# Two of every eight C products on VectorE, out of PSUM, and layer norm statistics on ScalarE, in a decoder layer with a Mamba scan

## The chip, the cores and the metric

The kernel runs on one core of one Trainium2 chip. The metric is the device time of one execution in microseconds (us). A core has a matrix engine (TensorE, PE in the profile, its weight loads PEld), VectorE (DVE), ScalarE (ACT), GpSimd (POOL) and SyncE (SP), which here only issues DMAs. Each engine works through its own queue in order; they meet through semaphores. SBUF and PSUM are the on-chip memories; PSUM has 8 banks of 512 f32 in each of 128 partitions.

## What is computed

A layer on x (64 sequences x 128 positions x 512): a Mamba mixer, banded attention gated by a context, and eight small experts of which two are chosen, each behind a layer norm and added to x.

```python
x = x + mamba(layernorm(x))
x = x + attention(layernorm(x), ctx)
x = x + experts(layernorm(x))

def layernorm(x): return (x - mean(x)) / sqrt(var(x) + 1e-5)

def mamba(x):                      # I = 1024 channels, N = 16 states
    h_in, gate = split(x @ in_proj_w.T)
    u  = silu(causal_conv4(h_in) + conv_b)
    ts, Bm, Cm = split(u @ x_proj_w.T)
    dt = softplus(ts @ dt_proj_w.T + dt_proj_b)
    # for each channel and state, over the 128 positions t:
    # h[t] = exp(dt[t] * A) * h[t-1] + dt[t] * u[t] * Bm[t]
    y  = sum_over_states(h * Cm) + D * u
    return (y * silu(gate)) @ out_proj_w.T
```

## The kernel before

Sequences go in pairs (a group g of GB = 2), 32 groups; a tile is 128 x 512 f32. The work is a software pipeline: one pass, `iteration(g, cur, nxt, p1, p2)`, carries four groups at once: the scans of group g (`cur`), norm, projections and convolution of group g+1 (`nxt`), output projection and attention of group g-1 (`p1`) and the experts of group g-2 (`p2`). Each engine has its own `iteration`, a list of calls written out by hand whose order is the order of the engine's queue; passes 2 to 29 run in a loop of two passes.

The scan is the core of it. A pass has 64 steps s, each for 128 channels (chunk `s // 8`) and two of the 16 states, over two sequences:

- ScalarE, `decays` (L462): two exponentials write exp(dt A) into PSUM bank `s % 2` (DAR = 2), all but column 0 of each sequence, which stays zero so that the scan restarts there. It waits for `h_done` of step s-2, whose decays had the bank.
- GpSimd, `times_b` (L300), the B product: writes dt u B into the ring slot `s % 8` of SBUF, once TensorE has used the slot (`hc_used`).
- VectorE, `scan` (L1454): reads the decays (PSUM) and the ring slot, and leaves the states in the ring slot.
- the C product, states times C, in place in the ring slot, `times_c`: on VectorE (L1439) for the steps in `DVE_C`, those with s % 8 in (1, 4, 7), 24 of 64; on GpSimd (L309) for the other 40.
- TensorE, `y_sum` (L1066): adds the ring slots, transposed, two steps at a time, into PSUM bank 2; `y_turn`, `y_back` and `out_proj` (L1087, L526, L1096) turn the gated result and project it.

Around that, VectorE has the four steps of the softplus and du (`soft_step`, L1423 to L1434), the convolution's taps (`conv`, L1582), the row maxima and products of attention (L1489, L1496, L1503, L1507, L1513), the router, and the statistics of the three layer norms a, t and e (`norm_stats`: bn_stats over 512, bn_aggr, add of eps; L1403 to L1408) for two tiles each. `hold` is a tiny copy that stands between a wait and an instruction that takes none. After the statistics GpSimd raises to the power -1/2 (`rstd`, L288), VectorE makes the shift (`shift`, L1413) and ScalarE normalises (L469).

ScalarE has besides the decays the copies out of PSUM, the softplus's exponential and logarithm, the attention's exponentials and the silus. Exponential, logarithm and silu lie in different function tables; a change of table is an ACT_TABLE_LOAD. PSUM bank 3 (PS_B) serves projections, gates and transposes in turn; banks 4 to 7 (PS_ATT) serve attention, output projection and experts. SyncE's queue loads x, the context (`context`), the weight pieces and the rows of B and C (`spread`).

Of the kernel before, what the change touches and what calls it, by code (L numbers as in the profile page):

```python
# [5 lines left out]
def decoder_layer(nc, x_d, ctx_d, w_in_d, conv_w_d, conv_b_d, w_xt_d, w_xbc_d, w_dt_d, dt_b_d, a_log_d,  # L6
# [9 lines left out]
    P = 128  # L16
# [22 lines left out]
    DVE_C = [s for s in range(64) if s % 8 in (1, 4, 7)]  # L39
# [7 lines left out]
    with stack:  # L47
# [33 lines left out]
        held = sb("held", [P, 1])  # L81
# [29 lines left out]
        ln_st = {k: sb("ln_st_" + k, [P, GB, 6]) for k in "ate"}  # L111
        ln_mv = {k: sb("ln_mv_" + k, [P, GB, 2]) for k in "ate"}
# [31 lines left out]
        st_open, bo_ps, bo_done, att_zero = sem("st_open"), sem("bo_ps"), sem("bo_done"), sem("att_zero")  # L144
# [54 lines left out]
        def _(sp):  # L199
# [78 lines left out]
        def _(pool):  # L278
            nc.gpsimd.memset(neg_half[:], -0.5).then_inc(const_done, 1)
            nc.gpsimd.memset(v_aug[:, :, :, DH + 1:32], 0.0).then_inc(att_zero, 1)  # L280
            nc.gpsimd.memset(v_aug[:, :, :, DH:DH + 1], 1.0).then_inc(att_zero, 1)
            nc.gpsimd.memset(nmax[:], 0.0).then_inc(att_zero, 1)
            pool.wait_ge(const_done, 1)
# [29 lines left out]
            def iteration(g, cur, nxt, p1, p2):  # L313
                if cur:
                    times_b(g, 0)
                    times_b(g, 1)
# [4 lines left out]
                if p1:  # L321
                    times_c(g - 1, 62)
                if cur:
                    times_b(g, 3)
                    times_c(g, 0)
                    times_b(g, 4)
                    times_b(g, 5)
                    times_c(g, 2)
                    times_b(g, 6)
                    times_c(g, 3)  # L330
                    times_b(g, 7)
                if nxt:
                    rstd("a", g + 1, 0, 2)
                if p1:
                    rstd("t", g - 1, 0)
                if cur:
                    times_b(g, 8)
                    times_c(g, 5)
                    times_b(g, 9)
                    times_c(g, 6)  # L340
                    times_b(g, 10)
                    times_c(g, 8)
                    times_b(g, 11)
                    times_c(g, 10)
                    times_b(g, 12)
                    times_c(g, 11)
                if p1:
                    rstd("t", g - 1, 1)
                if cur:
                    times_b(g, 13)  # L350
                    times_b(g, 14)
                    times_b(g, 15)
                    times_c(g, 13)
                    times_b(g, 16)
                    times_b(g, 17)
                    times_b(g, 18)
                    times_c(g, 14)
                    times_b(g, 19)
                    times_c(g, 16)
                    times_b(g, 20)  # L360
                    times_c(g, 18)
# [3 lines left out]
                    times_c(g, 19)  # L365
                    times_c(g, 21)
                    times_b(g, 24)
                    times_b(g, 25)
                    times_b(g, 26)
                    times_b(g, 27)  # L370
                    times_c(g, 22)
                    times_b(g, 28)
                    times_b(g, 29)
                    times_c(g, 24)
                    times_c(g, 26)
                    times_b(g, 30)
                    times_c(g, 27)
                    times_b(g, 31)
                    times_c(g, 29)
                    times_c(g, 30)  # L380
                    times_b(g, 32)
                    times_b(g, 33)
                    times_b(g, 34)
                    times_b(g, 35)
                    times_b(g, 36)
                    times_b(g, 37)
                    times_b(g, 38)
                    times_c(g, 32)
                    times_c(g, 34)
                    times_c(g, 35)  # L390
                    times_b(g, 39)
# [4 lines left out]
                    times_b(g, 43)  # L396
                    times_b(g, 44)
                    times_c(g, 38)
                    times_b(g, 45)
                    times_c(g, 40)  # L400
                    times_b(g, 46)
                    times_b(g, 47)
                    times_c(g, 42)
                    times_c(g, 43)
                    times_c(g, 45)
                    times_b(g, 48)
                    times_c(g, 46)
                    times_b(g, 49)
                    times_b(g, 50)
                    times_b(g, 51)  # L410
                    times_c(g, 48)
                    times_b(g, 52)
                    times_c(g, 50)
                    times_b(g, 53)
                    times_c(g, 51)
                    times_b(g, 54)
                    times_b(g, 55)
                    times_c(g, 53)
                    times_b(g, 56)
# [6 lines left out]
                    times_b(g, 61)  # L426
                    times_c(g, 58)
                    times_c(g, 59)
# [16 lines left out]
        def _(act):  # L445
# [7 lines left out]
            act.wait_ge(da_zeroed, 1)  # L453

            def decays(g, s):

                ic, r = s // RS, s % RS
                if s % (2 * RS) == 0:
                    act.wait_ge(dt_done, g * NQ + ic // 2 + 1)
                act.wait_ge(h_done, g * SG + s + 1)  # L460
                for n in (2 * r, 2 * r + 1):
# [3 lines left out]
                        scale=a_neg[:, ic, n:n + 1]).then_inc(da_done, 1)  # L465

# [16 lines left out]
            def step_size(j, q):  # L483

                reached(act, du_done, (j - 1) * NQ + q + 1)
                act.wait_ge(dt_ps, j * NQ + q + 1)
# [124 lines left out]
            def iteration(g, cur, nxt, p1, p2):  # L611
                j = g + 1
                if cur:
                    decays(g, 0)
                    decays(g, 1)
                    step_size(g, 3)
                if p2:
                    experts_norm(g - 2, 0)
                if cur:
                    decays(g, 2)  # L620
                if p2:
                    experts_norm(g - 2, 1)
                if cur:
                    decays(g, 3)
# [1285 lines left out]
```

## Time and profile before

| | us |
|---|---|
| median of 3 runs | 5537.23 |
| lowest, highest | 5533.24, 5540.6 |
| the profiled execution | 5533.42 |
| its span in the trace | 5531.6 |
| busy in the span: TensorE / VectorE / GpSimd / ScalarE | 4796.2 / 4955.4 / 4541.5 / 4058.8 |
| TensorE weight loads | 3435.7 |
| mean granted TensorE clock | 0.964 |

The profile is of one execution. Busy times of an engine can be set against the length of a stretch; an idle time is put down to the instruction whose semaphore came last. In names of groups the arrow points from the inputs to the output, and "x" gives the number of instructions. Consecutive instructions of an engine overlap a little, so the steps between starts are shorter than the durations.

### The profile page before, as it was taken

What the parts mean: (1) busy time and instruction counts of PE and PEld (TensorE: products, weight loads), DVE (VectorE), ACT (ScalarE), POOL (GpSimd) and SP (SyncE); (2) the same over time, 40 slices, a digit from 0 to 9 for tenths busy, and PEclk for the clock granted to TensorE, in tenths of its full rate; (3) what the DMA queues carried; (4) which work ended last, traced back from release to release, by engine and by line L of the source; (5) the groups of instructions that cost most, each with busy time, mean ns of one, the idle gap of its engine ahead of it and who ended that gap; (6) DMA issues with size and microseconds to landing.
All of it is one profiled execution on the core that took longest, in us unless ns stands there. A gap on an engine that the chain in (4) does not pass through costs nothing.

```text
span 5531.6 us, 139169 instructions
## 1 busy us (share of the span) xinstructions
PE 4796.2 (87%) x51012; PEld 3435.7 (62%) x51012; DVE 4955.4 (90%) x7075; ACT 4058.8 (73%) x7812; POOL 4541.5 (82%) x3464
## 2 busy tenths in 40 slices
PE   5788888988888988888989888989888988898876
PEld 3566666666666666666666666666666666666653
DVE  3999999999999999999999999999999999999972
ACT  3677777877777777777877777777777777777752
POOL 2988888888888888888888888888888888888870
PEclk8899999999999999999999999999999999999986
DMA  3211222221212221212221222221212221221100
GB/s 112 71 63 42 70 68 74 70 66 42 74 64 74 70 67 41 74 64 74 71 67 40 74 64 74 74 70 34 77 64 70 74 74 38 70 69 66 62 9 11
DMA packets 114693, 350.19 MB, mean 63 GB/s; under 512 B 13057, under 2 KB 14849, under 8 KB 113921
## 3 DMA queue, kind: packets, MB, share of 16 engines
q1 hardware_dynamic: 114048, 341.51, 19.0%
q8 instruction: 416, 6.82, 0.5%
q14 instruction: 229, 1.87, 0.1%
HBM read 323.64 MB, written 17.83 MB: 62 GB/s over the span
## 4 chain that ended last, share of the span: by engine, by line
PE 46%; DVE 18%; issue 15%; POOL 11%; ACT 7%; DVEq 1%; POOLq 0%; ACTq 0%
POOL ring L300 7%; PE ps L1066 7%; PE ps L1114 6%; DVE ring L1454 5%; PE ps L1096 5%; PE ps L982 4%; PE ps L957 4%; POOL ring L309 4%; PE ps L1134 3%; PE ps L1010 3%; DVE nmax L1489 3%; ACT ps L462 3%; DVE ring L1439 2%; DVE tmp L1423 2%; PE ps L1021 1%
## 5 line engine op out<-in xcount | busy, mean ns | idle before, releaser
L300 POOL TENSOR_TENSOR ring<-du,bc 128x512 f32<-128x512 f32 x2048 | 2741.9, 1356 | 577.7 <-PE ps L1066 352.3
L1454 DVE TENSOR_TENSOR_SCAN ring<-ps,ring 128x512 f32<-128x512 f32 x2048 | 2456.7, 1211 | 201.2 <-POOL ring L300 103.1
L462 ACT ACTIVATE ps<-delta,a_neg 128x254 f32<-128x254 f32 x4096 | 1761.5, 468 | 326.9 <-DVE ring L1454 320.9
L309 POOL TENSOR_TENSOR ring<-ring,bc 128x512 f32<-128x512 f32 x1280 | 1776.5, 1394 | 232.5 <-DVE ring L1454 230.6
L1066 PE MATMUL ps<-ident,ring 128*128 128x128 f32 x8192 | 1103.7, 282 | 73.7 <-DVE ring L1439 43.1
L1066 PEld LDWEIGHTS ps<-ident,ring 128*128 128x128 f32 x8192 | 962.9, 145 | 193.5 <-issue 119.1
L1439 DVE TENSOR_TENSOR ring<-ring,bc 128x512 f32<-128x512 f32 x768 | 755.4, 987 | 3.4
L592 ACT ACTIVATE probs_mem<-ps 128x768 f32<-128x768 f32 (+1 forms) x512 | 455.9, 911 | 176.0 <-PE ps L1010 174.4
L1134 PE MATMUL ps<-w_in,xt_a 128*128 128x256 f32 x2048 | 488.8, 394 | 12.8 <-DVE hc L1582 8.1
L1114 PE MATMUL ps<-xt_a,w_in 128*128 128x256 f32 x2048 | 476.6, 386 | 7.1 <-DVE hc L1582 4.1
L1096 PE MATMUL ps<-w_outp,yz 128*128 128x512 f32 x1024 | 462.5, 599 | 18.7 <-ACT yz L526 18.7
L1489 DVE TENSOR_REDUCE nmax<-ps 128x8 f32<-128x1280 f32 x256 | 380.7, 1487 | 78.4 <-PE ps L982 73.8
L1134 PEld LDWEIGHTS ps<-w_in,xt_a 128*128 128x128 f32 x2048 | 398.1, 200 | 68.4 <-DVE hc L1582 8.9
L1114 PEld LDWEIGHTS ps<-xt_a,w_in 128*128 128x128 f32 x2048 | 381.6, 191 | 76.7 <-issue 17.7
L1582 DVE SCALAR_TENSOR_TENSOR hc<-ps,conv_w,hc 128x254 f32<-128x254 f32 (+2 forms) x768 | 363.1, 473 | 62.2 <-ACT hc L537 42.7
L1096 PEld LDWEIGHTS ps<-w_outp,yz 128*128 128x128 f32 x1024 | 190.1, 191 | 227.9 <-issue 199.8
L982 PE MATMUL ps<-qk 32*32 32x160 f32 (+2 forms) x16384 | 296.2, 297 | 0.0
L1010 PE MATMUL ps<-qk 32*128 32x192 f32 (+1 forms) x4096 | 286.8, 397 | 0.0
L1021 PE MATMUL ps<-probs_mem,v_aug 128*32 128x192 f32 (+1 forms) x4096 | 229.8, 367 | 44.0 <-ACT probs_mem L592 43.9
L579 ACT ACTIVATE qk<-ps,b_qk 128x512 f32<-128x512 f32 x256 | 170.6, 678 | 125.6 <-PE ps L957 125.6
L957 PE MATMUL ps<-xb,w_qk 128*128 128x512 f32 x512 | 241.1, 593 | 2.8 <-ACT qk L579 1.3
L1010 PEld LDWEIGHTS ps<-qk 32*128 32x128 f32 x4096 | 186.3, 197 | 68.4 <-issue 63.1
(136 smaller groups left out, 6362.2 us busy)
## 6 DMA issues: line engine op xcount, KB each, us to landing
w_in<-in_w_in SPq DMA_DIRECT2D x256, 512.0 KB, 3.7
bc<-bc_rows SPq DMA_DIRECT2D x256, 512.0 KB, 4.1
x_new<-in_x SPq DMA_DIRECT2D x32, 512.0 KB, 6.2
x_res<-in_x SPq DMA_DIRECT2D x32, 512.0 KB, 5.5
enc<-in_ctx SPq DMA_DIRECT2D x64, 256.0 KB, 5.3
out<-x_att SPq DMA_DIRECT2D x32, 512.0 KB, 2.8
w_outp<-in_w_outp SPq DMA_DIRECT2D x1, 2048.0 KB, 8.0
bc_rows<-bc_sb SPq DMA_DIRECT2D x32, 32.0 KB, 1.5
```

Source lines behind the costliest of these rows:

```text
L300: nc.gpsimd.tensor_tensor(ring[:, s % RING, :].rearrange("p (n t) -> p n t", n=2), du[:, q % 2, (ic % 2) * NT:(ic % 2 + 1) * NT].rearrange ...
L309: nc.gpsimd.tensor_tensor(ring[:, s % RING, :], ring[:, s % RING, :], bc[:, s % RS, 2:4, :].rearrange("p a t -> p (a t)"), ALU.mult).then_ ...
L462: nc.scalar.activation(ps[:, s % DAR, (n % 2) * NT:(n % 2 + 1) * NT].rearrange("p (b t) -> p b t", b=GB)[:, :, 1:T], delta[:, ic, :].rearr ...
L982: last = nc.tensor.matmul(ps[32 * a:32 * a + 32, PS_ATT + hp, j * NEAR + lo:j * NEAR + hi], qk[r:r + 32, j, n * P + 32 * a:n * P + 32 * a ...
L1010: last = nc.tensor.matmul(ps[:, PS_ATT + hp, a * WIN + lo:a * WIN + hi], qk[r:r + 32, 2 + j, blk * P:(blk + 1) * P], qk[r:r + 32, j, at:at ...
L1066: last = nc.tensor.matmul(ps[:, PS_Y, b * T:(b + 1) * T], ring[:, t % RING, n * NT + b * T:n * NT + (b + 1) * T], ident[:], start=False, s ...
L1096: last = nc.tensor.matmul(ps[:, PS_ATT + b, :], yz[:, ic, b * T:(b + 1) * T], w_outp[:, ic, :], start=(ic == 0), stop=(ic == NI - 1))
L1114: last = nc.tensor.matmul(ps[:, PS_B, a * NT:(a + 1) * NT], w_in[:, slot, k, a * P:(a + 1) * P], xt_a[:, k, :], start=(k == 0), stop=(k == ...
L1134: last = nc.tensor.matmul(ps[:, PS_B, b * NT:(b + 1) * NT], xt_a[:, k, b * T:(b + 1) * T], w_in[:, slot, k, :], start=(k == 0), stop=(k == ...
L1439: nc.vector.tensor_tensor(ring[:, s % RING, :], ring[:, s % RING, :], bc[:, s % RS, 2:4, :].rearrange("p a t -> p (a t)"), ALU.mult).then_ ...
L1454: nc.vector.tensor_tensor_scan(ring[:, s % RING, :], ps[:, s % DAR, :], ring[:, s % RING, :], 0.0, ALU.mult, ALU.add).then_inc(h_done, 1)
L1489: nc.vector.tensor_reduce(nmax[:, n].rearrange("p j (a r) -> p a j r", r=32)[:, :, :, DH], ps[:, PS_ATT:PS_ATT + 4, 0:NJ * NEAR].rearrange ...
```

## The change

`DVE_C` becomes the steps with s % 8 in (3, 7), 16 of 64; GpSimd makes the other 48. For these 16 steps the scan leaves its states in the PSUM bank of the decays, over the decays, and VectorE's C product reads them there and writes the ring slot. Two steps later the bank takes decays again: ScalarE now waits for the C product (`hcd_done`) and first writes zeros back into the four first columns (`nc.scalar.copy`).

The statistics of the layer norms leave VectorE. The sum over a row comes as a second output (`accum_out`) of the additions that VectorE makes anyway (t and e), and for a from a pass of ScalarE over the tile (`total`). ScalarE squares the tile against its sum (`squares`; it writes into PS_B for a, into PS_ATT + b for t, into the context's buffer for e) and makes variance plus eps (`variance`). TensorE's first projection of attention waits for the squares of t, the load of the next context for those of e. The two copies in the router that only signal are made smaller. All `iteration` lists are written anew.

```diff
-    DVE_C = [s for s in range(64) if s % 8 in (1, 4, 7)]
+    DVE_C = [s for s in range(64) if s % 8 in (3, 7)]
...
             def context(i):
-                reached(sp, enc_used, i)
+                reached(sp, ln_aggr["e"], i)
...
             def decays(g, s):
...
+                if (s - DAR) % SG in DVE_C:
+
+                    reached(act, hcd_done, g * NDC + dvc(s - DAR + 1) if s >= DAR else (g - 1) * NDC + dvc(s - DAR + SG + 1))
+                    nc.scalar.copy(ps[:, s % DAR, :].rearrange("p (k t) -> p k t", t=T)[:, :, 0:1],
+                                   zeros[:].rearrange("p (k o) -> p k o", o=1)).then_inc(da_reset, 1)
                 act.wait_ge(h_done, g * SG + s + 1)
...
+            def total(j, b):
+                act.wait_ge(x_in, (j + 1) * 16)
+                nc.scalar.activation(x_new[:, b, :], x_new[:, b, :], ACT.Identity,
+                                     accum_out=ln_sum["a"][:, b:b + 1]).then_inc(ln_stat["a"], 1)
+
+            def squares(use, g, b):
+
+                i = g * GB + b
+                if use == "a":
+                    reached(act, yz_done, (g - 1) * NI)
+                    reached(act, gate_done, g * NQ)
+                    if b:
+                        act.wait_ge(ln_aggr["a"], i)
+                src = {"a": x_new, "t": x_res, "e": x_att}[use]
+                act.wait_ge({"a": ln_stat["a"], "t": x1_done, "e": x2_done}[use], i + 1)
+                nc.scalar.activation({"a": ps[:, PS_B, :], "t": ps[:, PS_ATT + b, :], "e": enc[:]}[use], src[:, b, :], ACT.Square,
+                                     scale=-float(H), bias=ln_sum[use][:, b:b + 1],
+                                     accum_out=ln_var[use][:, b:b + 1]).then_inc(ln_aggr[use], 1)
+
+            def variance(use, g, b):
+                act.wait_ge(ln_aggr[use], g * GB + b + 1)
+                nc.scalar.activation(ln_rs[use][:, b:b + 1], ln_var[use][:, b:b + 1], ACT.Identity,
+                                     scale=1.0 / H ** 3, bias=eps[:]).then_inc(ln_eps[use], 1)
...
                     if n == 0:
                         pe.wait_ge(xb_done, i + 1)
-                        pe.wait_ge(x1_done, g * GB)
+                        pe.wait_ge(ln_aggr["t"], g * GB)
...
             def times_c(g, s):
                 dve.wait_ge(h_done, H0 + 1 + g * SG + s)
-                nc.vector.tensor_tensor(ring[:, s % RING, :], ring[:, s % RING, :],
+                nc.vector.tensor_tensor(ring[:, s % RING, :], ps[:, s % DAR, :],
...
-                nc.vector.tensor_tensor_scan(ring[:, s % RING, :], ps[:, s % DAR, :], ring[:, s % RING, :], 0.0,
+                state = ps[:, s % DAR, :] if s in DVE_C else ring[:, s % RING, :]
+                nc.vector.tensor_tensor_scan(state, ps[:, s % DAR, :], ring[:, s % RING, :], 0.0,
...
-                nc.vector.tensor_tensor(x_res[:, b, :], ps[:, PS_ATT + b, :], x_res[:, b, :], ALU.add).then_inc(x1_done, 1)
+                nc.vector.scalar_tensor_tensor(x_res[:, b, :], ps[:, PS_ATT + b, :], 1.0, x_res[:, b, :], ALU.mult, ALU.add,
+                                               accum_out=ln_sum["t"][:, b:b + 1]).then_inc(x1_done, 1)
```

In VectorE's list of scans 47 to 56, for instance, the C products stood as 47, 49 (after scan 53), 52 (after 54) and 55; now 47, 51 and 55 each stand right behind their own scan.

The order on VectorE in a pass of the loop, from scan 2 on. The scan reads as SCALAR_TENSOR_TENSOR here; ISA and REGISTER_ALU rows prepare or make a wait. Before:

```order
L1454 SCALAR_TENSOR_TENSOR ring<-ps,ring 128x512 [waits dbx_done,da_done]
L1452 REGISTER_ALU
L1454 SCALAR_TENSOR_TENSOR ring<-ps,ring 128x512 [waits dbx_done,da_done]
L1482 ISA
L1403 BN_STATS ln_st_a<-x_new 128x6 [waits x_in]
L1404 ISA
L1399 COPY held<-neg_half 128x1 [waits ln_stat_a]
L1406 BN_AGGR ln_mv_a<-ln_st_a 128x2
L1408 TENSOR_SCALAR ln_rs_a<-ln_mv_a 128x1 [waits ln_aggr_a]
L1452 ISA
L1454 SCALAR_TENSOR_TENSOR ring<-ps,ring 128x512 [waits dbx_done,da_done]
```

Now:

```order
L1532 SCALAR_TENSOR_TENSOR ring<-ps,ring 128x512 [waits dbx_done,da_done]
L1529 ISA
L1532 SCALAR_TENSOR_TENSOR ps<-ps,ring 128x512 [waits dbx_done,da_done]
L1515 REGISTER_ALU
L1516 TENSOR_TENSOR ring<-ps,bc 128x512 [waits h_done]
L1529 ISA
L1532 SCALAR_TENSOR_TENSOR ring<-ps,ring 128x512 [waits dbx_done,da_done]
L1529 REGISTER_ALU
L1532 SCALAR_TENSOR_TENSOR ring<-ps,ring 128x512 [waits dbx_done,da_done]
L1545 REGISTER_ALU
L1546 REGISTER_ALU [waits xres_in]
L1547 SCALAR_TENSOR_TENSOR x_res,ln_sum_t<-ps,x_res 128x512 [waits outp_ps]
```

Between scans 3 and 4 the statistics of x_new are gone and a C product out of PSUM stands there, right behind its scan, which writes ps.

The order on ScalarE at the softplus's logarithm and the experts' silu, between the decays of steps 8 and 9. Before:

```order
L512 ACT_TABLE_LOAD
L512 ACTIVATE lnv<-soft 128x512
L609 ACT_TABLE_LOAD
L609 ACTIVATE probs_mem<-ps 128x256
L460 REGISTER_ALU
L462 ACT_TABLE_LOAD
L462 ACTIVATE ps<-delta,a_neg 128x2x127 x2
```

Now, with the reset of the bank that step 7's states had:

```order
L556 ACT_TABLE_LOAD
L556 ACTIVATE lnv<-soft 128x512
L507 ACTIVATE ln_rs_a<-ln_var_a,eps 128x1
L198 REGISTER_ALU
L477 COPY ps<-zeros 128x4
L479 REGISTER_ALU
L481 ACT_TABLE_LOAD
L481 ACTIVATE ps<-delta,a_neg 128x2x127 x2
```

The logarithm's load is followed by the exponentials' own load at once; the silu's load, which shared its change of table with it, now stands some rows further on with another pair.

The order on GpSimd in the same stretch, B products (ring<-du,bc) and C products (ring<-ring,bc). Before, from the B product of step 4 on:

```order
L299 REGISTER_ALU
L300 TENSOR_TENSOR ring<-du,bc 128x512
L299 REGISTER_ALU
L300 TENSOR_TENSOR ring<-du,bc 128x512
L309 TENSOR_TENSOR ring<-ring,bc 128x512
L299 REGISTER_ALU
L300 TENSOR_TENSOR ring<-du,bc 128x512
L309 TENSOR_TENSOR ring<-ring,bc 128x512
L299 REGISTER_ALU
L300 TENSOR_TENSOR ring<-du,bc 128x512
```

Now, from the B product of step 4 on too:

```order
L303 REGISTER_ALU
L304 TENSOR_TENSOR ring<-du,bc 128x512
L313 TENSOR_TENSOR ring<-ring,bc 128x512
L303 REGISTER_ALU
L304 TENSOR_TENSOR ring<-du,bc 128x512
L303 REGISTER_ALU
L304 TENSOR_TENSOR ring<-du,bc 128x512
L303 REGISTER_ALU
L304 TENSOR_TENSOR ring<-du,bc 128x512
L303 REGISTER_ALU
L304 TENSOR_TENSOR ring<-du,bc 128x512
L313 TENSOR_TENSOR ring<-ring,bc 128x512 x4
```

Before, B and C products alternate; now four B products stand ahead of four C products.

## Rows read from the trace of the kernel before

**Rows 1.** The page: busy time and share of the span, by engine.

```profile
PE 4796.2 (87%) x51012; PEld 3435.7 (62%) x51012; DVE 4955.4 (90%) x7075; ACT 4058.8 (73%) x7812; POOL 4541.5 (82%) x3464
```

**Rows 2.** Engines by stretch: start:end us, length, busy us (instructions), clock, DMA.

```profile
1009.80:1087.30 77.50, 66.64 (x569) 48.61 (x569) 72.47 (x92) 65.23 (x124) 65.10 (x49) 0.98 0.29 95
1087.30:1175.10 87.80, 80.67 (x1034) 57.44 (x1034) 82.61 (x131) 62.41 (x124) 77.68 (x62) 1.00 0.12 39
2000.00:3000.00 1000.00, 889.77 (x9716) 638.23 (x9716) 930.88 (x1334) 763.82 (x1470) 855.65 (x653) 0.98 0.20 65
```

**Rows 3.** The chain of waits, first and last of 25 pieces: start us, us.

```profile
927.63 6.97 PE ps L1096 x16
4897.35 6.97 PE ps L1096 x16
```

**Rows 4.** Waits between 1000 and 4968 us: us in total, times, longest us.

```profile
PE ps L928 <- DVE nmax L1489: 45.9, 72, 1.0
DVE ring L1454 <- POOL ring L300: 70.1, 93, 1.3
DVE ring L1454 <- ACT ps L462: 67.0, 69, 1.9
POOL ring L300 <- PE ps L1066: 278.2, 179, 4.4
POOL ring L309 <- DVE ring L1454: 174.7, 109, 2.6
ACT ps L462 <- DVE ring L1454: 212.0, 155, 2.0
```

**Rows 5.** Groups by line; behind the bar busy us, mean ns of one, then idle.

```profile
L300 POOL TENSOR_TENSOR ring<-du,bc 128x512 f32<-128x512 f32 x2048 | 2741.9, 1356 | 577.7 <-PE ps L1066 352.3 <-DVE du L1434 225.4
L1454 DVE TENSOR_TENSOR_SCAN ring<-ps,ring 128x512 f32<-128x512 f32 x2048 | 2456.7, 1211 | 201.2 <-POOL ring L300 103.1 <-ACT ps L462 94.2 <-issue 0.3
L309 POOL TENSOR_TENSOR ring<-ring,bc 128x512 f32<-128x512 f32 x1280 | 1776.5, 1394 | 232.5 <-DVE ring L1454 230.6
L1439 DVE TENSOR_TENSOR ring<-ring,bc 128x512 f32<-128x512 f32 x768 | 755.4, 987 | 3.4
L1423 DVE SCALAR_TENSOR_TENSOR tmp<-tmp,soft 128x512 f32<-128x512 f32 x128 | 174.6, 1364 | 19.6 <-ACT tmp L506 19.6
L1503 DVE TENSOR_TENSOR o_sb<-ps,o_sb 128x512 f32<-128x512 f32 x128 | 81.3, 675 | 3.7 <-PE ps L1040 3.7
L1513 DVE SCALAR_TENSOR_TENSOR x_att<-ps,b_ct,x_res 128x512 f32<-128x512 f32 x64 | 46.9, 733 | 4.1 <-PE ps L1050 4.1
```

**Rows 6.** Single lines of VectorE and GpSimd: duration ns min/median/max.

```profile
L1439 DVE TENSOR_TENSOR ring<-ring,bc x768: 657/693/1791, 106.5 to 5374.2; 128x512 f32<-128x512 f32 x192
L1503 DVE TENSOR_TENSOR o_sb<-ps,o_sb x128: 664/677/692, 320.2 to 5499.6; 128x512 f32<-128x512 f32 x128
L300 POOL TENSOR_TENSOR ring<-du,bc x2048: 1253/1275/1831, 99.5 to 5371.5; 128x512 f32<-128x512 f32 x187
L309 POOL TENSOR_TENSOR ring<-ring,bc x1280: 1253/1277/1772, 105.5 to 5373.9; 128x512 f32<-128x512 f32 x183
```

**Rows 7.** VectorE in order of time, statistics of one tile: start us, us.

```profile
1090.20 0.14 DVE L1399 COPY held<-neg_half 128x1 f32<-128x1 f32 x1
...
1091.36 0.69 DVE L1423 SCALAR_TENSOR_TENSOR tmp<-tmp,soft 128x512 f32<-128x512 f32 x1
```

**Rows 8.** ScalarE in order of time: start us, us.

```profile
1093.83 0.21 ACT L605 ACTIVATE small<-small 128x16 f32<-128x16 f32 x1 [4.07 <-DVE small L1538]
1093.95 0.85 ACT L462 ACTIVATE ps<-delta,a_neg 128x254 f32<-128x254 f32 x2
1094.82 1.28 ACT L512 ACT_TABLE_LOAD   x1
1096.11 0.63 ACT L512 ACTIVATE lnv<-soft 128x512 f32<-128x512 f32 x1
...
1100.56 0.80 ACT L469 ACTIVATE xb<-x_res,ln_nm_t,ln_rs_t 128x512 f32<-128x512 f32 x1
```

More of the change, by code:

```diff
@@ L614, in iteration @@
                     decays(g, 0)
+                    step_size(g, 3)
+                if nxt:
+                    total(j, 0)
+                if cur:
                     decays(g, 1)
-                    step_size(g, 3)
+                if nxt:
+                    total(j, 1)
+                if cur:
+                    decays(g, 2)
                 if p2:
@@ L619, in iteration @@
                 if cur:
-                    decays(g, 2)
+                    decays(g, 3)
                 if p2:
@@ L635, in iteration @@
                     decays(g, 6)
+                if nxt:
+                    squares("a", g + 1, 0)
                 if p2:
                     experts_x(g - 2, 1)
+                if nxt:
+                    squares("a", g + 1, 1)
                 if cur:
                     decays(g, 7)
+                if p1:
+                    squares("t", g - 1, 0)
+                if cur:
+                    soft_one(g, 2)
+                if nxt:
+                    variance("a", g + 1, 0)
+                if p1:
+                    variance("t", g - 1, 0)
+                if cur:
+                    decays(g, 8)
+                    soft_ln(g, 2)
+                if nxt:
+                    variance("a", g + 1, 1)
+                if cur:
+                    decays(g, 9)
                 if p2:
@@ L666, in iteration @@
                     attention(g, p2, 0, "v")
+                if cur:
+                    decays(g, 13)
                 if nxt:
@@ L730, in iteration @@
                     decays(g, 29)
+                    skip_term(g, 5)
+                    decays(g, 30)
+                    soft_one(g, 3)
+                    decays(g, 31)
                 if p1:
@@ L755, in iteration @@
                 if cur:
-                    skip_term(g, 5)
                     decays(g, 36)
+                if p1:
+                    attention(g, p2, 1, "v")
+                if cur:
                     decays(g, 37)
+                    decays(g, 38)
+                    decays(g, 39)
                 if nxt:
@@ L778, in iteration @@
                     attention(g, p2, 1, "exp", 0)
+                    squares("e", g - 1, 0)
                 if cur:
-                    decays(g, 44)
                     decays(g, 45)
-                    skip_term(g, 6)
                 if p1:
@@ L808, in iteration @@
                 if cur:
-                    decays(g, 51)
+                    decays(g, 48)
+                if p1:
+                    attention(g, p2, 1, "exp", 4)
+                if cur:
+                    decays(g, 49)
+                if p1:
+                    attention(g, p2, 1, "exp", 5)
+                if cur:
+                    decays(g, 50)
                 if nxt:
@@ L839, in iteration @@
                     decays(g, 57)
+                if p1:
+                    attention(g, p2, 1, "wide")
+                if nxt:
+                    step_size(j, 0)
+                if cur:
+                    decays(g, 58)
+                if nxt:
+                    soft_exp(j, 0)
+                if cur:
+                    decays(g, 59)
                 if nxt:
@@ L1684, in iteration @@
                     scan(g, 19)
+                    times_c(g, 19)
+                    y_step(g, 1)
+                    scan(g, 20)
                 if nxt:
```

583 lines of the change are left out of this document (271 added, 312 removed).

## The prediction

> **What bounds the kernel now.** I read the busy shares first: VectorE 4955 us of 5532, GpSimd 4542, ScalarE 4059, TensorE 4796 [rows 1]. Then the period: the long output projection comes once a pass, 24 passes lie between 927.63 and 4897.35, so one pass takes 165.4 us [rows 3]. The steady stretch from 2000 to 3000 us gives the load of a pass (times 0.1654): VectorE 154.0, TensorE 147.2, GpSimd 141.5, ScalarE 126.3 [rows 2]. VectorE is busy 93.1% of a pass and is what bounds it, closely followed.
>
> A pass has two halves. In the first (77.5 us) VectorE has 72.5, TensorE 66.6, ScalarE 65.2, GpSimd 65.1; in the second (87.8 us) VectorE has 82.6 and TensorE 80.7 [rows 2]. VectorE's own idle time before scans is 2.9 us a pass for GpSimd's B product and 2.8 for ScalarE's decays (70.1 and 67.0 over 24); GpSimd waits 11.6 for ring slots and 7.3 for scans, ScalarE 8.8 for scans, TensorE 1.9 for the row maxima [rows 4]. So the others mostly wait at VectorE's pace.
>
> **VectorE.** Today 24 C products of 987 ns; a product with one operand in PSUM takes 675 [rows 5]. The shortest C product takes 657 and the longest 1791, the PSUM one 664 to 692, and GpSimd's products stretch in the same way, from 1253 to 1831 [rows 6]: two engines hold each other up when VectorE reads two operands from SBUF. The change leaves 16 products, all with the state in PSUM: 24 x 0.987 - 16 x 0.675 = 12.9 us less. The statistics of a tile take 1.16 us (1090.20 to 1091.36) [rows 7], six a pass: 7.0 less. Added: sums written out by four additions; the nearest prices are 0.06 (733 against 675 [rows 5]) and a small instruction's 0.14 [rows 7], at least nothing: 0 to 0.6, I take 0.4. The scan's output moves to PSUM in 16 of 64 scans. No row shows VectorE writing 512 elements there; reading there costs 677 against 693 in the medians [rows 6], and the small gap 733 - 675 bounds it above: -0.3 to +1.0, taken as 0, since a scan is paced by its recurrence at 1211 [rows 5]. VectorE: 154.0 - 12.9 - 7.0 + 0.4 = 134.5. The router's two copies swapped for smaller ones are nothing.
>
> The Trainium skill speaks against the PSUM operand: "VectorE: DVE Perf Modes", section "The TRN2 errata", gives a VectorE read from PSUM 62 cycles more fixed cost than one from SBUF, by my estimate from its figures 1.0 us a pass. The medians 677 and 693 [rows 6] don't show it; by it the pass of VectorE would be 135.5 and still last.
>
> **GpSimd.** Eight more C products at the undisturbed 1.277 [rows 6]: +10.2. Its means exceed its medians by 64 x 0.081 + 40 x 0.117 = 9.9 a pass [rows 5, 6], time in which VectorE holds it up. VectorE's C products exceed 675 by 24 x 0.312 = 7.5, the first softplus step, which reads two SBUF operands too, by 4 x 0.689 = 2.8 [rows 5], the other steps by less; so I give two thirds of the 9.9, 6.6, to the C products, and it goes. GpSimd: 141.5 + 10.2 - 6.6 = 145.1, between 141.8 (all goes) and 151.7 (nothing goes).
>
> **ScalarE.** Added in a pass: 16 resets of the first decay column, 0.12 (start to start) to 0.21 each [rows 8], at 0.17: 2.7. Two sums at 0.63 and six squares at 0.80 like the passes over 512 elements [rows 8]: 6.1. Six variances at 0.21: 1.3. Table loads: the order in the loop has 24 for two passes before and 30 now, three more a pass at 1.29 (1094.82 to 1096.11) [rows 8]: 3.9. ScalarE: 126.3 + 14.0 = 140.3; reading the accumulators out is not in any row, nothing to 8 x 0.21 = 1.7 more.
>
> The Trainium skill, "ScalarE: Activation LUTs", section "What ACT_TABLE_LOAD costs", puts a drain of some 1.4 us behind each load; that would make it 8.0 for the three. The row has the next activation start 1.29 after the load began [rows 8], so I keep 3.9.
>
> **TensorE** keeps its work, 147.2. The added waits: the projection of the first batch waits for both squares of the mixer's sum, since they overwrite its two banks (before: for the additions only); behind it the rest of attention is queued. The prefetch of the context waits for the squares of the experts' input, with a weight piece and the spread rows behind it on SyncE's queue. Both are issued some ten or more scans ahead of their use and I price them at 0, at most 0.8 each, the length of a squares pass [rows 8], if the cover is gone.
>
> **The sum.** The order of load is now TensorE 147.2, GpSimd 145.1, ScalarE 140.3, VectorE 134.5. What comes last is no longer one engine. Two ways to a period: (a) TensorE as full as VectorE was, 147.2 / 0.931 = 158.1. (b) By halves with the old placing: first half ScalarE 65.2 + 7.0 = 72.2, at the old fullness 72.5 / 77.5 = 77.2 us; second half TensorE 80.7, at 82.6 / 87.8 = 85.8 us; together 163.0. The new order moves work between halves but four engines within 9% of each other leave less room to absorb waits. I take the middle, 160.5: 4.9 us a pass, 32 passes (2048 scans of 64) [rows 5], 157 us. Against the profiled execution of 5533.4 (span 5531.6): 5376; the median lies 3.8 above that, so **5380**.
>
> **Rivals.**
> (1) More: half of TensorE's idle 18.2 us goes too, since part of it is waits for VectorE (the row maxima [rows 4]). 147.2 + 9.1 = 156.3 a pass, 291 less: 5246. Against it: GpSimd would be 93% and ScalarE 90% full.
> (2) Less: the halves don't even out, 163.0 a pass, 77 less: 5460. For it: ScalarE gains most load and sits in the half where it becomes last.
> (3) The change doesn't do what it says: a C product with bc in SBUF is still held up. Then GpSimd has 151.7, and 151.7 / 0.931 = 162.9: 5457. The row of 664 to 692 [rows 6] speaks against it.
> (4) Slower: the two decay banks. A scan in PSUM keeps its bank until the C product has read it, and only then come the reset and both exponentials for the scan two ahead. The chain scan, decays, scan gets 0.68 + 0.17 = 0.85 longer in 16 places, and where ScalarE stands at a reset, everything behind it on its queue stands too: copies for TensorE, the exponentials of attention. Before, two exponentials (0.85 [rows 8]) hid behind the scan in between (1.21 [rows 5]); now 0.17 + 0.85 leaves about 0.2 for two hand-overs. What is uncovered adds to 160.5; from 4.9 / 16 = 0.31 us a product the kernel is slower. At 0.55 it is 8.8 a pass, 169.3: 5662. For it: at scans 47 to 55 of the new order nothing else lies between. Against it: VectorE has 26 us of room in 160.5.
>
> **Chances.** Forecast 0.48; (1) 0.14; (2) 0.17; (3) 0.03; a tie between (2) and (4), within 0.2% (about what a measurement of this kernel can tell from no change), 0.06; (4) 0.12. Faster 0.82, same 0.06, slower 0.12. The range reaches from just beyond (1) to the edge of no change, 5235 to 5525; it leaves out (4) and a tail of (1). The unknown costs lie inside: GpSimd's ends 141.8 to 151.7, at 93.1%, give 152 to 163 a pass.
>
> **What would show it.** C products at 0.67 to 0.70 with a short maximum; GpSimd's two means near 1.30; fifteen table loads a pass; VectorE's share near 84%, TensorE's 92%; the long projections 160.5 apart. (4) shows as ScalarE's wait before the reset and VectorE's before scans <- ScalarE well over 2.8 us a pass. The forecast is wrong if the PSUM scan costs over 1.3, or if ScalarE waits more than before at decays and reset together.

## The result, and the profile after

The changed kernel takes 5381.8 us (5376.4 to 5387.6, four runs), before 5535.2 (5531.2 to 5540.6): ratio 0.9722, 95% interval 0.9706 to 0.9739. It is faster by 2.8%, and within 2 us of the forecast. Several of the forecast's steps were wrong all the same, and the runs below show which.

The page of the changed kernel, span and busy time by engine, against [rows 1]:

```profile
span 5385.8 us, 140112 instructions
PE 4741.3 (88%) x51012; PEld 3415.9 (63%) x51012; DVE 4558.6 (85%) x6051; ACT 4440.9 (82%) x9121; POOL 4640.2 (86%) x3722
```

VectorE has lost 397 us, ScalarE has gained 382, GpSimd only 99 although it makes eight more C products a pass. The length of a pass is again the distance between two long projections in the chain of waits of the changed kernel (start us, us), four passes apart:

```profile
4207.13 3.65 PE ps L1219 x16
...
4847.82 3.65 PE ps L1219 x16
```

640.69 / 4 = 160.2 us, where [rows 3] gave 165.4. The loads per thousand microseconds between 1000 and 4000 us, the view of [rows 2]:

```profile
sum 3000.00, PE 2733.41 PEld 1975.59 DVE 2647.92 ACT 2598.14 POOL 2716.39; mean PE 911.14 PEld 658.53 DVE 882.64 ACT 866.05 POOL 905.46
```

Times 0.1602, a pass holds TensorE 146.0, GpSimd 145.1, VectorE 141.4, ScalarE 138.7 us. The four lie within some 5%. TensorE's busy time has fallen too, from 4796.2 to 4741.3 us for the same 51012 matmuls; nothing in the change takes work off it.

The groups of the changed kernel that answer to [rows 5] (busy us, mean ns of one, then idle before and its releasers):

```profile
L304 POOL TENSOR_TENSOR ring<-du,bc 128x512 f32<-128x512 f32 x2048 | 2630.2, 1299 | 369.3 <-PE ps L1151 262.8
L1532 DVE TENSOR_TENSOR_SCAN ring<-ps,ring 128x512 f32<-128x512 f32 x1536 | 1851.4, 1212 | 285.3 <-ACT ps L481 251.3
L313 POOL TENSOR_TENSOR ring<-ring,bc 128x512 f32<-128x512 f32 x1536 | 2012.0, 1320 | 90.7 <-DVE ring L1532 87.8
L1532 DVE TENSOR_TENSOR_SCAN ps<-ps,ring 128x512 f32<-128x512 f32 x512 | 623.2, 1217 | 49.4 <-ACT ps L481 43.6
L1516 DVE TENSOR_TENSOR ring<-ps,bc 128x512 f32<-128x512 f32 x512 | 350.2, 684 | 9.9
L1500 DVE SCALAR_TENSOR_TENSOR tmp<-tmp,soft 128x512 f32<-128x512 f32 x128 | 236.1, 1845 | 26.7 <-ACT tmp L550 25.7
```

VectorE's C product fell from 987 to 684 ns, GpSimd's B product from 1356 to 1299 and its C product from 1394 to 1320. A scan that writes PSUM takes 1217, one that writes SBUF 1212. The first softplus step (now L1500) got longer, 1845 against 1364. The same lines one by one (ns min/median/max), as in [rows 6]:

```profile
L1516 DVE TENSOR_TENSOR ring<-ps,bc x512: 665/691/693, 111.0 to 5223.7; 128x512 f32<-128x512 f32 x171
L304 POOL TENSOR_TENSOR ring<-du,bc x2048: 1252/1272/1807, 101.7 to 5221.0; 128x512 f32<-128x512 f32 x187
```

The longest C product is 693 ns, before 1791: no GpSimd product holds one up any more.

The waits of the changed kernel between 1000 and 4841 us, 24 passes (us in total, times, longest us):

```profile
PE ps L1013 <- DVE nmax L1554: 110.2, 98, 3.0
DVE ring L1532 <- ACT ps L481: 184.4, 239, 3.3
DVE ps L1532 <- ACT ps L481: 28.2, 43, 1.5
ACT ps L477 <- DVE ring L1516: 86.5, 120, 2.3
ACT ps L481 <- DVE ring L1532: 127.2, 120, 3.0
```

VectorE now waits 8.9 us a pass for decays ((184.4 + 28.2) / 24) where it waited 2.8 [rows 4], and ScalarE stands 3.6 at the new reset. TensorE's wait for the row maxima has risen from 1.9 to 4.6. ScalarE's waits at decays and reset together are 213.7 us, before 212.0 at the decays alone.

**Where the time went.** From the first scan to the last, 164.65 us a pass became 159.9, 151.5 us in 32 passes; what follows the last scan became 4.8 us longer (158.6 to 163.4). Seen from TensorE, the span is 145.8 us shorter, 90.9 of them idle time and 54.9 busy time.

### The profile page after: what moved, and what is told of

Same layout as the page of the kernel before. It is cut to its first block and busy times, and to the rows that moved or that the text cites. A ratio compares the mean times of both kernels' runs of the same rounds, so it can differ in the third digit from the quotient of the medians.

```text
span 5385.8 us, 140112 instructions
## 1 busy us (share of the span) xinstructions
PE 4741.3 (88%) x51012; PEld 3415.9 (63%) x51012; DVE 4558.6 (85%) x6051; ACT 4440.9 (82%) x9121; POOL 4640.2 (86%) x3722
## 5 line engine op out<-in xcount | busy, mean ns | idle before, releaser
L304 POOL TENSOR_TENSOR ring<-du,bc 128x512 f32<-128x512 f32 x2048 | 2630.2, 1299 | 369.3 <-PE ps L1151 262.8
L1532 DVE TENSOR_TENSOR_SCAN ring<-ps,ring 128x512 f32<-128x512 f32 x1536 | 1851.4, 1212 | 285.3 <-ACT ps L481 251.3
L313 POOL TENSOR_TENSOR ring<-ring,bc 128x512 f32<-128x512 f32 x1536 | 2012.0, 1320 | 90.7 <-DVE ring L1532 87.8
L1151 PEld LDWEIGHTS ps<-ident,ring 128*128 128x128 f32 x8192 | 950.5, 144 | 225.4 <-issue 117.7
L1532 DVE TENSOR_TENSOR_SCAN ps<-ps,ring 128x512 f32<-128x512 f32 x512 | 623.2, 1217 | 49.4 <-ACT ps L481 43.6
L1199 PE MATMUL ps<-xt_a,w_in 128*128 128x256 f32 x2048 | 478.1, 387 | 9.4 <-DVE hc L1647 4.1
L1181 PE MATMUL ps<-w_outp,yz 128*128 128x512 f32 x1024 | 480.3, 607 | 3.6 <-issue 2.2
L1516 DVE TENSOR_TENSOR ring<-ps,bc 128x512 f32<-128x512 f32 x512 | 350.2, 684 | 9.9
L1067 PE MATMUL ps<-qk 32*32 32x160 f32 (+2 forms) x16384 | 314.2, 316 | 1.7 <-issue 1.7
L1095 PE MATMUL ps<-qk 32*128 32x192 f32 (+1 forms) x4096 | 273.6, 382 | 0.0
L1500 DVE SCALAR_TENSOR_TENSOR tmp<-tmp,soft 128x512 f32<-128x512 f32 x128 | 236.1, 1845 | 26.7 <-ACT tmp L550 25.7
```

Source lines behind the costliest of these rows:

```text
L304: nc.gpsimd.tensor_tensor(ring[:, s % RING, :].rearrange("p (n t) -> p n t", n=2), du[:, q % 2, (ic % 2) * NT:(ic % 2 + 1) * NT].rearrange ...
L313: nc.gpsimd.tensor_tensor(ring[:, s % RING, :], ring[:, s % RING, :], bc[:, s % RS, 2:4, :].rearrange("p a t -> p (a t)"), ALU.mult).then_ ...
L1067: last = nc.tensor.matmul(ps[32 * a:32 * a + 32, PS_ATT + hp, j * NEAR + lo:j * NEAR + hi], qk[r:r + 32, j, n * P + 32 * a:n * P + 32 * a ...
L1151: last = nc.tensor.matmul(ps[:, PS_Y, b * T:(b + 1) * T], ring[:, t % RING, n * NT + b * T:n * NT + (b + 1) * T], ident[:], start=False, s ...
L1181: last = nc.tensor.matmul(ps[:, PS_ATT + b, :], yz[:, ic, b * T:(b + 1) * T], w_outp[:, ic, :], start=(ic == 0), stop=(ic == NI - 1))
L1199: last = nc.tensor.matmul(ps[:, PS_B, a * NT:(a + 1) * NT], w_in[:, slot, k, a * P:(a + 1) * P], xt_a[:, k, :], start=(k == 0), stop=(k == ...
```

## The experiments

My theory was the forecast's: the C product out of PSUM ends the mutual hold-up of VectorE and GpSimd, the statistics give the rest, and VectorE was what bound the kernel before. The rival: another engine set the pace, and the loads of VectorE and GpSimd count only through what waits for them. The first four kernels take the change apart, the next six load one engine at a time, and the last two move the hand-over of the bank and the split of the products. All kernels compute the same outputs; those named "more" do extra work whose result nobody reads.

**The states back in SBUF**, without and with the reset and its wait. Two lines of the changed kernel; in the first kernel, `states_sbuf`, the five lines of the reset in `decays` go too:

```diff
-                nc.vector.tensor_tensor(ring[:, s % RING, :], ps[:, s % DAR, :],
+                nc.vector.tensor_tensor(ring[:, s % RING, :], ring[:, s % RING, :],
-                state = ps[:, s % DAR, :] if s in DVE_C else ring[:, s % RING, :]
+                state = ring[:, s % RING, :]
```

> The changed kernel with the 16 states back in SBUF: the scan writes the ring slot, VectorE's C product reads it there, and the reset and ScalarE's wait for the C product are gone. Theory (contention): VectorE's C product rises from 0.684 to about 0.99 us (some 5 us a pass), GpSimd's two means from 1.30 to about 1.35 (some 5 us a pass); the period grows by 2 to 4 us from 160.2, time 5450 to 5510. Rival (the bank chain costs what the PSUM operand saves): the chain reset, decays, scan is 0.85 shorter in 16 places, the two cancel, time within 15 us of 5382.

> As the one before, states in SBUF, but the reset and ScalarE's wait for the C product kept. Theory (the bank chain is covered, as VectorE has room): within 10 us of the one without them. Rival (the chain costs up to 0.85 us in 16 places): 50 to 300 us slower than the one without them.

Measured: `states_sbuf` 5520.1 us, ratio 0.9979 (0.9969 to 0.9988); `states_sbuf_reset` 5545.0, ratio 1.0022 (1.0012 to 1.0032). The page and two groups of `states_sbuf`:

```profile
PE 4801.6 (87%) x51012; PEld 3443.4 (62%) x51012; DVE 4779.1 (87%) x6051; ACT 4396.1 (80%) x8609; POOL 4909.2 (89%) x3722
L304 POOL TENSOR_TENSOR ring<-du,bc 128x512 f32<-128x512 f32 x2048 | 2770.4, 1368 | 294.2 <-PE ps L1146 194.3 <-DVE du L1506 99.4
L1511 DVE TENSOR_TENSOR ring<-ring,bc 128x512 f32<-128x512 f32 x512 | 688.4, 1345 | 9.9
```

The same 16 products take 1345 ns instead of 684, and GpSimd is busy 269 us longer with the same instructions. Nearly the whole gain, 138 us between these two kernels, hangs on where one operand lies. The loss is larger than expected, 5520 against 5450 to 5510, and so is the hold-up: 1345 ns where the kernel before had 987, so that part of what the operand saves is a hold-up that only the new order and split have. The hand-over of the decay bank costs a further 25 us (5520 to 5545) when the states gain nothing by it, more than the 10 that the theory allowed and less than the rival's 50.

The 138 us are not all waits. Of the 131.4 us between the two spans, TensorE's idle time has 71.1 (715.6 against 644.5) and its busy time 60.3 (4801.6 against 4741.3), for the same matmuls. The granted clock of its rows was 0.955 in `states_sbuf` and 0.965 in the changed kernel. A lower clock beside a longer busy time fits, but no run separates what the clock does from the rest.

**The statistics back on VectorE** (`stats_back`), and with it also the states in SBUF and no reset (`only_split`, which leaves of the change its order and the two products of eight). The statistics stand behind the additions of their tile, which lose their second output; the three ScalarE functions return at once, and TensorE and the context's load wait as in the kernel before:

```diff
+                nc.vector.bn_stats(ln_st[use][:, b, :], src[:, b, :]).then_inc(ln_stat[use], 1)
...
+                nc.vector.bn_aggr(ln_mv[use][:, b, :], ln_st[use][:, b, :]).then_inc(ln_aggr[use], 1)
...
+                nc.vector.tensor_scalar(ln_rs[use][:, b:b + 1], ln_mv[use][:, b, 1:2], EPS, None, ALU.add).then_inc(ln_eps[use], 1)
```

> The changed kernel with the layer norm statistics back on VectorE (bn_stats, bn_aggr and add of eps as before, placed behind the additions), none on ScalarE. Theory (no engine alone sets the period; VectorE at 142 of 160 has room for 7 us): between 10 us faster and 40 us slower than 5382. Rival 1 (ScalarE's 9 us a pass are on the path): 100 us or more faster. Rival 2 (VectorE still bounds through its waits): 7 us a pass, 220 us slower.

> Both undone: states in SBUF without reset, statistics on VectorE. What is left of the change is two of eight C products and the new order. Theory: VectorE near 154 again less 8 C products (147), GpSimd at 151 with the contention back: period 163 to 165, time 5470 to 5530. Rival (the gain is the order's): it stays within 30 us of 5382.

Measured: `stats_back` 5389.0, ratio 0.9738 (0.9722 to 0.9754); `only_split` 5514.3, ratio 0.9966 (0.9954 to 0.9977). So the change comes apart as: order and split 19 us, PSUM operand 125 (5514.3 to 5389.0), statistics 7, and these last can't be told from nothing, since the intervals overlap. With the states in SBUF, moving the statistics costs 6 instead (5514.3 to 5520.1). How the PSUM operand reaches the end of the program shows in TensorE's waits over the whole run, first of `only_split`, then of `stats_back`:

```profile
PE ps L1013 <- DVE nmax L1576: 211.1, 118, 4.4
PE ps L1151 <- DVE ring L1539: 73.5, 59, 1.7
```

```profile
PE ps L1018 <- DVE nmax L1581: 128.3, 126, 3.0
```

TensorE waits 83 us less for the row maxima of attention, which VectorE makes between its scans; all its waits together fall from 722 to 626. The other 30 us are again TensorE's busy time (4786.9 to 4757.2). A product held up makes VectorE late at the work that TensorE waits for. But GpSimd is relieved as well: the operand takes 214 us of busy time off VectorE (4893.4 to 4679.4) and 243 off GpSimd (4900.9 to 4657.6), and no run takes only one of the two.

**One engine loaded at a time, in the changed kernel.** VectorE gets six `bn_stats` a pass over a constant (`dve_more`), ScalarE 24 small activations (`act_more`), GpSimd six small products (`pool_more`), and TensorE the first of four matmuls of `h_in` twice (`pe_more`):

```diff
+                if s % 10 == 5:
+                    nc.vector.bn_stats(pad_st[:], w_outp[:, 0, :])
```

```diff
+                if s % 8 == 5:
+                    reached(act, pad_done, (g * 8 + s // 8) * 3)
+                    for i in range(3):
+                        nc.scalar.activation(pad[:, 16 * i:16 * i + 16], ident[:, 0:16], ACT.Identity).then_inc(pad_done, 1)
```

```diff
+                if s % 10 == 5:
+                    nc.gpsimd.tensor_tensor(pad[:], pad[:], pad[:], ALU.mult)
```

```diff
-                    for k in range(KH):
+                    for n in range(-1, KH):
+                        k = max(n, 0)
...
+                                                xt_a[:, k, :], start=(k == 0), stop=(n in (-1, KH - 1)))
```

> The changed kernel with six bn_stats over a constant weight tile added to a pass on VectorE (behind scans 5, 15, ... 55), 0.60 each from start to start: 3.6 us a pass, 116 us in all, whose result nobody reads. Theory (the next in load sets the pace, TensorE and GpSimd; VectorE has 20 us of room): a third of it or less, 0 to 40 us. Rival (VectorE still sets it through the chain scan, C product, reset): 80 us or more.

> The changed kernel with 24 tiny activations added to a pass on ScalarE (three behind the decays of steps 5, 13, ... 61), about 0.13 each: 3.1 us a pass, 100 us in all. Theory: ScalarE follows, 20 to 60 us. Rival (ScalarE sets the pace through the decays): 80 us or more.

> The changed kernel with six 64-wide products of a constant added to a pass on GpSimd (behind the B products of steps 5, 15, ... 55), 0.6 each: 3.6 us a pass, 115 us in all. Theory (GpSimd, 90% busy and first in the chain of waits, sets the pace with TensorE): 60 to 115 us. Rival (TensorE alone): under 30 us.

> The changed kernel with the first of the four weight rows multiplied twice in the convolution's projection (the first result is overwritten): eight 128x256 products of f32 a pass at 0.45, 3.6 us a pass, 115 us in all. Theory (TensorE, 91% busy, sets the pace with GpSimd): 60 to 115 us. Rival (GpSimd alone): under 30 us.

Measured, ratio to before: VectorE 0.9777 (0.9761 to 0.9794), ScalarE 0.9768 (0.9752 to 0.9784), GpSimd 0.9777 (0.9761 to 0.9794), TensorE 0.9918 (0.99 to 0.9935). The added groups, of `dve_more`, `act_more` and `pe_more` in turn (`pe_more` has 2560 of the last, the changed kernel 2048 and 478.1 us):

```profile
L1538 DVE BATCH_NORM_STATS2 pad_st<-w_outp 128x6 f32<-128x512 f32 x192 | 128.1, 667 | 0.0
```

```profile
L491 ACT ACTIVATE pad<-ident 128x16 f32<-128x16 f32 x768 | 106.2, 204 | 0.0
```

```profile
L1200 PE MATMUL ps<-xt_a,w_in 128*128 128x256 f32 x2560 | 587.8, 385 | 8.1 <-DVE hc L1648 4.1 <-ACT gate_t L595 2.6 <-ACT xt_a L574 0.8
```

Against the changed kernel's 0.9722, VectorE's 128 us cost 30, ScalarE's 106 cost 25, GpSimd's 58 cost 30 (each difference has some 13 us either way), and TensorE's 110 us cost 108. GpSimd's lands at its rival's bound (under 30, expected 60 to 115); the other three lie in the ranges of the theory. Only TensorE passes its work on whole, or nearly: its busy time rose by 124 us in all, VectorE's by 99, so that by these totals the shares are 0.9 and 0.3. TensorE's work was added in one place, ahead of a projection that others wait for, the work of the others was spread over the pass; a second place on TensorE was not tried.

**The same in the kernel before** (`before_dve_more`, `before_pe_more`; the edits are those above).

> The kernel before with the same six bn_stats a pass on VectorE (99 us of busy time in the changed kernel, where they cost 27). Theory (VectorE bounded the kernel before): 70 to 120 us slower than before, 5605 to 5655. Rival (TensorE bounded it already): under 40 us.

> The kernel before with the same doubled first products on TensorE (124 us of busy time in the changed kernel, where they cost 103). Theory (VectorE bounded it, TensorE had 18 us of room a pass): 20 to 70 us slower than before. Rival (TensorE bounded it already): 90 us or more.

Measured: 1.0088 (1.0072 to 1.0105) and 1.0205 (1.0188 to 1.0222): VectorE's 127.6 us of added work cost 49 us, TensorE's 110.5 cost 113. These are the runs that my theory fails on: I had expected 70 to 120 from VectorE and 20 to 70 from TensorE. The engine that was 93% busy passed 0.4 of its load on, the one that was 89% busy all of it. The page of the kernel before had a sign of it, the shares of the chain of work that ended last:

```profile
PE 46%; DVE 18%; issue 15%; POOL 11%; ACT 7%; DVEq 1%; POOLq 0%; ACTq 0%
```

**The decay bank uncovered** (`c_late`). Each of the 16 C products stands behind the scan that follows its own, so the bank is handed over one scan later; the other 15 calls go as the one shown, and no work is added. Only 12 of them move: those of steps 15, 27 and 31 stand there in the changed kernel too, and 63, the last of the pass, stays behind its own scan.

```diff
+                if s - 1 in DVE_C:
+                    times_c(g, s - 1)
+                if s == 63 and 1:
+                    times_c(g, 63)
...
-                    times_c(g, 3)
+                    pass
```

> The changed kernel with VectorE's 16 C products each behind the next scan instead of their own (63 at the pass's end). The bank's chain C product, reset, two exponentials then starts 1.2 us later and nothing covers it: VectorE waits about 1.1 us before 15 scans, 16 us a pass. Theory (the chain costs only what VectorE's room of 18 us and its slope of a quarter let through): 80 to 250 us slower than 5382. Rival (ScalarE stands at the reset and holds up TensorE's copies too): 300 us or more.

Measured: 5781.5, ratio 1.0452 (1.0435 to 1.047), 400 us over the changed kernel, more than the 80 to 250 expected, or 1.04 for each of the 12 products that moved. ScalarE's and VectorE's waits in it, over the whole run (in the changed kernel 134.5 us at the reset and 294.9 before scans):

```profile
ACT ps L477 <- DVE ring L1516: 565.1, 386, 6.0
```

```profile
L1532 DVE TENSOR_TENSOR_SCAN ring<-ps,ring 128x512 f32<-128x512 f32 x1536 | 1856.3, 1214 | 662.1 <-ACT ps L481 641.3 <-POOL ring L304 8.3 <-issue 3.7
```

With the scans into PSUM, VectorE's wait for decays is 734.9 us in `c_late`. The fourth rival's mechanism is real, and larger than the 0.85 that the forecast gave as its whole length. VectorE was busy 78% of the span, and its room did not help: the scans wait one after another, and room elsewhere does not shorten a chain.

**Five of sixteen C products on VectorE** (`dve_20`: 20 instead of 16 of 64), to see whether the fuller GpSimd holds the kernel.

```diff
-    DVE_C = [s for s in range(64) if s % 8 in (3, 7)]
+    DVE_C = [s for s in range(64) if s % 8 in (3, 7) or s % 16 == 5]
...
+                if s in DVE_C and s % 4 != 3:
+                    times_c(g, s)
```

> A version that may be better: VectorE makes 20 of 64 C products out of PSUM, those with s % 16 == 5 too, right behind their scans; GpSimd makes 44. By the slopes measured (VectorE 0.27, GpSimd 0.52, ScalarE 0.31 of what is added or taken): a pass +0.7 - 2.7 + 0.2 = -1.8 us, 56 us less, 5325. Rival (TensorE sets the pace and the places of the four are no good for the bank's chain): within 15 us of 5382 or slower.

Measured: 5401.7, ratio 0.976 (0.9744 to 0.9776), 20 us slower than the changed kernel where a gain of 56 was expected. The page and GpSimd's first group:

```profile
PE 4752.0 (88%) x51012; PEld 3418.7 (63%) x51012; DVE 4599.6 (85%) x6179; ACT 4453.8 (82%) x9249; POOL 4466.2 (82%) x3594
L304 POOL TENSOR_TENSOR ring<-du,bc 128x512 f32<-128x512 f32 x2048 | 2606.0, 1290 | 508.0 <-PE ps L1153 351.4 <-DVE du L1513 155.5
```

GpSimd is busy 174 us less and waits 139 us more (508.0 against 369.3): it used the room to wait, most of it for ring slots that TensorE empties. ScalarE's wait at the reset rose too, from 134.5 to 206.0 us (640 resets instead of 512), so the run does not say which of the two took the gain. (The trace is of the slowest of the four executions, 5424.6 us.) None of my kernels beats the changed one.

## Why the prediction was right, and where it was not

**The C product: right.** 684 ns against 675 forecast, and 693 at most. `states_sbuf` shows the other side, 1345. The row on which the step stood, a VectorE addition out of PSUM that was never longer than 692 [rows 6], carried over. The 62 cycles more of a PSUM read, in the Trainium skill's "VectorE: DVE Perf Modes", section "The TRN2 errata", don't show: the median is 691 here and was 693 from SBUF [rows 6].

**The scan into PSUM: right**, 5 ns more (1217 against 1212), 0.1 us a pass.

**GpSimd: right.** 145.1 forecast, 145.1 measured. The contention share too: 4909.2 - 4640.2 = 269 us between `states_sbuf` and the changed kernel is 8.4 a pass for 16 products of 1345 ns, against 6.6 forecast for 24 of 987.

**ScalarE: right**, 138.7 against 140.3. Its own rows, resets, table loads, sums with the new read-out of the accumulator, and variances, in the changed kernel:

```profile
L477 ACT COPY ps<-zeros 128x4 f32<-128x4 f32 x512 | 84.7, 165 | 134.9 <-DVE ring L1516 134.5
L481 ACT ACT_TABLE_LOAD x189 | 242.5, 1283 | 3.3
L488 ACT ACTIVATION_READ_ACCUMULATOR x_new<-x_new x64: 185/187/193, 19.6 to 4907.7; 128x1 f32 x64
L507 ACT ACTIVATE ln_rs_a<-ln_var_a,eps x64: 277/281/292, 21.9 to 4924.3; 128x1 f32<-128x1 f32 x64
```

The resets are 0.165 (0.17 forecast), the variances 0.28 (0.21), the read-out 0.19 for each of eight sums, 1.5 a pass, near the upper bound that was given; the squares took 0.69 instead of 0.80, which makes up for part of it. All table loads together are 479, fifteen a pass. Nothing stands behind a load: the logarithms, each of which follows one, sat idle 1.4 us before all 128 of them:

```profile
L556 ACT ACTIVATE lnv<-soft 128x512 f32<-128x512 f32 x128 | 80.7, 631 | 1.4
```

The drain of 1.4 us a load, in the Trainium skill's "ScalarE: Activation LUTs", section "What ACT_TABLE_LOAD costs", is not in this trace.

**VectorE: off by 6.9 us**, 141.4 instead of 134.5. The largest part, 4.4, is the softplus. Its later steps in the changed kernel (in the kernel before the four steps took 466.3 us together, now 236.1 for L1500 and these):

```profile
L1511 DVE TENSOR_TENSOR du<-delta,u 128x512 f32<-128x512 f32 x128 | 126.4, 988 | 0.0
L1503 DVE SCALAR_TENSOR_TENSOR delta<-delta,tmp 128x512 f32<-128x512 f32 x128 | 123.5, 965 | 0.0
L1507 DVE TENSOR_TENSOR delta<-delta,lnv 128x512 f32<-128x512 f32 x128 | 121.9, 952 | 2.7 <-ACT lnv L556 2.7
```

607.9 - 466.3 = 141.6 us, over 32 passes 4.4. They read two operands from SBUF, as the C product did; the forecast freed VectorE of the hold-up only where it removed it, and let it grow nowhere. It is not simply that GpSimd is fuller: the four steps took 473.2 us in `only_split`, where GpSimd is busy 4900.9, and 552.3 in `stats_back`, where it is busy 4657.6. What decides is not shown; which GpSimd products stand beside the steps changes with each kernel. A second part is the statistics. The 1.16 us of [rows 7] is start to start and holds gaps between small instructions, while a load is busy time: by `stats_back`, whose VectorE is busy 4679.4 us, they were worth about (120.8 + 55.6 for its shorter softplus + 10.5 for the accumulators) / 32 = 5.8 a pass, not 7.0. Of the last 1.3, the scans' busy time has 0.6 (2474.6 us against 2456.7); the rest I can't place.

**"VectorE bounds the kernel": wrong.** This is the step that failed. The forecast read it from the busy share and from the waits, and the added loads deny it (0.4 against 1.0, in the kernel before). The Trainium skill, "Perfetto Trace Analysis", section "Identifying the Most-Contended Engine", takes the engine of highest occupancy as the one to improve, which would have misled here as it misled me; of TensorE it says that its matmul busy share does not tell how close it is to its limit, and here the engine with the lower share was the one that passed its load on. So the 12.9 us a pass priced on VectorE's C products paid 19 and 125 us over 32 passes, 4.5 a pass (the 19 with the new order in them), in good part through the waits of TensorE, and the 5.8 of the statistics paid next to nothing: 7 us in all, by intervals that overlap.

**Why the sum came out.** Way (a) divided TensorE's 147.2 by a fullness, and TensorE is indeed what a pass is measured by; its fullness rose from 89% to 91%. Its load was kept at 147.2 without a second look and measured 146.0; over the run its busy time fell by 54.9 us, more than a third of the 145.8 that the span lost. At 91.1% the forecast's load would have given 161.6 a pass. That the fullness reached was between VectorE's old 93% and the halves' estimate was a middle taken between two ways, not a derivation. The ways lay 4.9 us a pass apart, 157 us in all, so that coming within 2 us of the total is partly luck, and VectorE's part in it had the wrong reason.

**Rivals.** (3) fell with the 693. (1) fell: TensorE's idle time is 14.2 us a pass and not 9.1. (2) was the nearer one, 163.0 against 160.2. (4), the decay bank, happened as described, but small: the hand-over cost 25 us in the form without its gain, 0.05 a product, where the forecast had the kernel slower from 0.31. Its signs were poor ones: VectorE's wait before scans rose from 2.8 to 8.9 a pass, and ScalarE's waits at decays and reset together are just over those of before (213.7 against 212.0 us), which the forecast named as proof that it was wrong; the time fell all the same. It stayed small where the C product stands ahead of the next scan, as 13 of the 16 do; `c_late` gives its price without that. The reason given against it, VectorE's room, was no reason.

**Not settled.** What of the 19 us of `only_split` is the new order and what the two products of eight was not run apart, nor was the lower fullness of TensorE divided between its many small waits. Open too are why TensorE is busy for less time with the same matmuls, and how much of the operand's gain comes by VectorE and how much by GpSimd.

## What to carry to other kernels

Where a VectorE instruction reads two tensors from SBUF beside a busy GpSimd, try one of them in PSUM: here the instruction halved (1345 to 684 ns) and GpSimd's got shorter too. Before pricing a load that is taken off an engine, find which engine sets the pace, by adding a known load to each in turn; the busiest one may pass on less than half. When a buffer gets one more reader before it is free, write that reader first thing behind the writer.

## What the runs showed of the hardware that I had not expected

A VectorE instruction with two SBUF operands can be held up over several GpSimd products in a row, not by one alone. VectorE and GpSimd of the changed kernel in order of time (start us, us), around the longest L1500:

```profile
5145.43 9.22 DVE L1500 SCALAR_TENSOR_TENSOR tmp<-tmp,soft 128x512 f32<-128x512 f32 x1
5145.50 1.26 POOL L304 TENSOR_TENSOR ring<-du,bc 128x512 f32<-128x512 f32 x1
...
5146.73 1.26 POOL L313 TENSOR_TENSOR ring<-ring,bc 128x512 f32<-128x512 f32 x1
5147.97 3.69 POOL L304 TENSOR_TENSOR ring<-du,bc 128x512 f32<-128x512 f32 x3
...
5151.63 1.25 POOL L313 TENSOR_TENSOR ring<-ring,bc 128x512 f32<-128x512 f32 x1
5152.85 1.25 POOL L304 TENSOR_TENSOR ring<-du,bc 128x512 f32<-128x512 f32 x1
...
5154.58 1.21 DVE L1532 TENSOR_TENSOR_SCAN ring<-ps,ring 128x512 f32<-128x512 f32 x1
```

Seven GpSimd products of 1.25 us stand back to back, to 5154.10, and VectorE's instruction ends 0.55 us after the last of them, where GpSimd pauses. The Trainium skill, "SBUF — State Buffer", section "Who interferes with whom", has a VectorE instruction with two SBUF inputs contend with GpSimd's reads, and one with a single SBUF input not; 1345 against 684 ns agrees with both. The row above shows the loser losing several times in turn. All L1500 (ns min/median/max):

```profile
L1500 DVE SCALAR_TENSOR_TENSOR tmp<-tmp,soft x128: 693/1748/9221, 93.3 to 5145.4; 128x512 f32<-128x512 f32 x128
```

The median of 1.75 is 1.06 over the shortest, a hold-up of about one product. What decides who is held up, and how often, was not tried.
